# A two-layer attention and mixture-of-experts kernel: routing products of 128 columns, and one token buffer in the first expert stage

## The chip, the cores and the metric

The kernel runs on one core of a Trainium2 chip. The metric is the device time of one execution in microseconds (us). TensorE (PE in the profile) has a clock that is granted to it at one of two levels, 1.2 or 2.4 GHz; the profile prints the granted clock as a share of the full one (0.50 or 1.00). A measurement of this kernel is repeated with the same program, and the three runs before lie within 1.9 us of each other.

## What is computed

The input is `x`, 4 x 512 = 2048 tokens of 512 numbers, and a context of 4 x 512 x 128. Four sublayers are added to the tokens one after the other:

```python
x = x + graph_attention(ctx_512, layernorm(x), ...)
x = x + ffn(layernorm(x), gate, gate_up_proj, down_proj)          # 32 experts, top 4
x = x + attention(q=layernorm(x), k=ctx_512, v=ctx_512)           # 32 heads of 16
x = x + moe(layernorm(x), w_cls, bias, w_gate_up, w_down)         # 32 real + 32 empty experts, top 8, capacity 256
```

In each of the two expert sublayers a token's normalised row is multiplied with a routing matrix (512 x 32 in the first, 512 x 64 in the second), a softmax gives scores, the largest 4 (8) are kept and normalised. Each chosen expert computes `silu(x Wg) * (x Wu)` and a product with its down matrix, and the weighted results are summed into the token.

## The kernel before, in words

The program (`two_layers`) is a chain of stages with a barrier over all engines between them: graph attention (`g_` in tile names), first expert sublayer (`sparse_ffn` with prefix `f`: a stage `route`, tiles `fr_`, and a stage `experts`, tiles `f_`), `attention_prepare` (`p_`), `attention` (`a_`), the second expert sublayer (`sr_` and `s_`), and `copy_out`. Inside a stage each engine has its own instruction list, written out by hand, and waits on semaphores. SP issues plain DMAs, POOL (GpSimd) issues the indirect ones. The running sum of the tokens lives in a DRAM tensor `tokens`.

**`route`** works on 16 tiles of 128 tokens, in 4 groups of 4. DVE computes statistics, ACT and DVE normalise, PE transposes a tile in four pieces (L863, bank `xtb`), ACT copies it to SBUF (L904, `xT`), and PE multiplies the four pieces with the four slices of the routing matrix (L870): the stationary operand is the token tile, the moving one is `gate_sb[:, c, :]` with E = 32 or 64 columns, and the result is the tile's logits in bank `lg`. In the trace such a float32 product of the program shows as two records, a transpose as one. PE's list is: transposes of tile t, then products of tile t-1. After the products of a group DVE takes the maxima (`maxima(g)`, L971), ACT the exponentials, DVE chooses (`choose(g)`) and works out places (`places(g)`). DVE's list in the middle is

```python
maxima(0); maxima(1); choose(0); maxima(2); choose(1); places(0)
maxima(3); choose(2); places(1); choose(3); places(2); weights(); places(3)
```

and then, in the first sublayer, how many tiles of 128 each expert gets (`tiles_of`, at least one), the number of its first tile (`first`), and a table of the expert of each of the 96 tiles, which goes through a PE transpose into row `table`. The last result is `ids`, the token numbers of each tile's 128 places (L1102). Beside that SP stores the normalised rows (`x_rows`), loads the weights of the first four experts and, in the first sublayer only, fills a second DRAM tensor `tokens_odd` with zeros (L816, 4.6 MB).

**`experts`** goes over 96 tiles (first sublayer) or 64 (second, two for each expert: `static`). POOL gathers the rows of a tile by `ids` (L1204), six tiles ahead. PE, ACT and DVE transpose them, do the up product, the activation, the down product; ACT copies the result into one of four buffers `y` (L1311). POOL waits for it (`y_ready`) and for the scatter two tiles back (`added[j % 2]`), and issues an indirect DMA that adds the 128 rows of `y` to DRAM (L1219). Tokens in the tiles of one expert are distinct; those of two experts can be the same, and two such additions must not be under way at once. The first sublayer avoids it with two targets: even tiles are added to `tokens`, odd ones to `tokens_odd`. The second has one target and waits at each even tile (a new expert) for the scatter just before. ACT may write `y` of tile j once the scatter of tile j-4 has landed.

**`attention_prepare`** loads `tokens` and `tokens_odd` in four pairs (L1431, L1432), DVE adds them (L1496), takes statistics (L1499), SP stores the sum back to `tokens` (L1437). After the mean and deviation of all 16 tiles it normalises (L1513), and PE, ACT and DVE transpose each tile and split it into three bf16 parts that SP stores.

Of the kernel before, what the change touches and what calls it, by code (L numbers as in the profile page):

```python
# [11 lines left out]
P = 128  # L12
RING = 2
FP32 = mybir.dt.float32
BF16 = mybir.dt.bfloat16
I32 = mybir.dt.int32
# [601 lines left out]
def sparse_ffn(nc, tokens, tokens_odd, gate, sel_bias, gate_up, down, K, capacity, pre):  # L618
# [5 lines left out]
    RE = 4  # L624
# [4 lines left out]
    with ExitStack() as stack:  # L629
        def sb(name, shape, dt=FP32):  # L630
# [5 lines left out]
            "table": sb("table", [1, 2 * P + NE], I32),  # L636
# [7 lines left out]
        route(nc, tokens, tokens_odd, gate, sel_bias, gate_up, down, x_rows, kept, K, capacity, n_tiles, RE, pre + "r_")  # L644
        experts(nc, tokens, tokens_odd, gate_up, down, x_rows, kept, capacity, n_tiles, RE, pre + "_")


def route(nc, tokens, tokens_odd, gate, sel_bias, gate_up, down, x_rows, kept, K, capacity, n_tiles, RE, pre):
# [17 lines left out]
    XTR = 4  # L666
    ids, table_i, wgu, wd = kept["ids"], kept["table"], kept["wgu"], kept["wd"]
# [3 lines left out]
    with ExitStack() as stack:  # L671
# [25 lines left out]
        gate_sb = sb("gate", [P, DC, E])  # L697
# [30 lines left out]
        passed = sb("passed", [P, ER])  # L728
        expert_of = sb("expert_of", [P, 1])
# [7 lines left out]
        def logits(t):  # L737
            return lg_bank[t // G][:, t % G * E:(t % G + 1) * E]

        def group_logits(g):  # L740
            return lg_bank[g][:, 0:G * E].rearrange("p (t e) -> p t e", t=G)

        def group_pos(g):
            return lg_bank[g][:, 256:256 + G * ER].rearrange("p (t e) -> p t e", t=G)
# [31 lines left out]
        N_CONST = 10  # L776
        with nc.Block() as block:

            @block.gpsimd
            def _(pool):  # L780
# [18 lines left out]
                pool.memset(zeros_e[:, :], 0.0).then_inc(consts, 1)  # L799
                pool.iota(my_slot[:, :], [[P, n_tiles]], base=1, channel_multiplier=1, allow_small_or_imprecise_dtypes=True).then_inc(consts, 1)  # L800

            @block.sync
            def _(sp):
                for g in range(NG):
# [4 lines left out]
                    elif g == 0:  # L809
                        sp.dma_start(gate_sb[:, :, :], gate.rearrange("(c p) e -> p c e", p=P)).then_inc(gate_loaded, 16)  # L810
# [294 lines left out]
def experts(nc, tokens, tokens_odd, gate_up, down, x_rows, kept, capacity, n_tiles, RE, pre):  # L1105
# [17 lines left out]
    with ExitStack() as stack:  # L1123
# [53 lines left out]
        with nc.Block() as block:  # L1177
# [20 lines left out]
            def _(pool):  # L1198
# [9 lines left out]
                for j in range(AHEAD):  # L1208
                    gather(j)
# [761 lines left out]
```

## Time and profile before

| | us |
|---|---|
| median of 3 runs | 2397.76 (2395.94 to 2397.82) |
| the profiled execution, its own time | 2393.21 |
| its span in the trace | 2391.6 |
| PE busy in the span | 1884.6 (79%) |
| DVE busy | 1558.2 (65%) |
| ACT busy | 1113.1 (47%) |
| POOL busy | 575.8 (24%) |
| mean granted clock of TensorE | 0.883 |

A time in the trace counts from the start of the span. A row of the timeline gives start, duration, engine, line, operation, written and read tiles, shape, number of merged instructions, and in brackets how long the engine was idle before and what ended that. A row of a table by stretch gives the stretch, its length, then for each engine the busy time and the number of instructions, then the granted clock, the busy share of the DMA engines and GB/s.

### The profile page before, as it was taken

What the parts mean: (1) busy time and instruction counts of PE and PEld (TensorE: products, weight loads), DVE (VectorE), ACT (ScalarE), POOL (GpSimd) and SP (SyncE); (2) the same over time, 40 slices, a digit from 0 to 9 for tenths busy, and PEclk for the clock granted to TensorE, in tenths of its full rate; (3) what the DMA queues carried; (4) which work ended last, traced back from release to release, by engine and by line L of the source; (5) the groups of instructions that cost most, each with busy time, mean ns of one, the idle gap of its engine ahead of it and who ended that gap; (6) DMA issues with size and microseconds to landing.
All of it is one profiled execution on the core that took longest, in us unless ns stands there. A gap on an engine that the chain in (4) does not pass through costs nothing. (4 is left out here: it accounts for less than half of the span.)

```text
span 2391.6 us, 34851 instructions
## 1 busy us (share of the span) xinstructions
PE 1884.6 (79%) x8270; PEld 919.9 (38%) x8271; DVE 1558.2 (65%) x3296; ACT 1113.1 (47%) x2022; POOL 575.8 (24%) x679
## 2 busy tenths in 40 slices
PE   1898867888567999999982159888889638999994
PEld 0444424444264555555541112222222324454442
DVE  5988969888665555555556257777777394555552
ACT  1988849888432222222222316666666532222221
POOL 3000030001102455454540201111111103444441
PEclk9899877999757999999995569999999768999997
DMA  4101121001364778888558741111111345898984
GB/s 134 39 37 42 35 103 45 36 37 36 107 230 100 172 184 211 210 190 197 106 87 276 130 74 50 53 49 49 49 49 45 128 146 148 229 228 227 232 215 109
DMA packets 207120, 288.47 MB, mean 121 GB/s; under 512 B 83168, under 2 KB 121440, under 8 KB 205920
## 3 DMA queue, kind: packets, MB, share of 16 engines
q1 hardware_dynamic: 168464, 190.16, 26.0%
q0 software_dynamic: 38544, 97.02, 20.3%
q8 instruction: 46, 0.75, 0.1%
q14 instruction: 66, 0.54, 0.1%
HBM read 208.64 MB, written 82.28 MB: 122 GB/s over the span
## 5 line engine op out<-in xcount | busy, mean ns | idle before, releaser
L1829 DVE TENSOR_REDUCE a_negmax<-a_m 128x1 f32<-128x512 f32 x512 | 327.8, 685 | 86.3 <-PE a_m L1694 84.6
L1783 ACT ACTIVATE a_prob<-a_s 128x1024 f32<-128x1024 f32 x256 | 260.2, 1020 | 142.7 <-PE a_s L1705 136.3
L1694 PE MATMUL a_m<-a_kT,a_qT 112*128 (+1 forms) x512 | 198.2, 398 | 115.6 <-DMA a_kT<-k_parts 63.9
L1253 PE MATMUL f_gu_bank<-f_wgu,f_xT 128*128 x768 | 271.2, 496 | 15.7 <-issue 12.1
L354 PE MATMUL g_pt<-g_ident,g_p 128*128 128x128 f32 x1024 | 185.2, 311 | 95.8 <-ACT g_p L460 94.4
L1253 PE MATMUL s_gu_bank<-s_wgu,s_xT 128*128 128x512 f32 x512 | 232.7, 597 | 2.3 <-ACT s_xT L1305 1.6
L354 PEld LDWEIGHTS g_pt<-g_ident,g_p 128*128 128x128 f32 x1024 | 127.2, 155 | 239.2 <-issue 153.5
L460 ACT ACTIVATE g_p<-g_e,g_emin 128x512 f32<-128x512 f32 x256 | 184.2, 719 | 66.0 <-DVE g_emin L554 65.7
L1253 PEld LDWEIGHTS f_gu_bank<-f_wgu,f_xT 128*128 128x128 f32 x768 | 141.5, 191 | 156.3 <-issue 79.7
L544 DVE SCALAR_TENSOR_TENSOR g_l<-g_tb,g_s,g_h 128x512 f32<-128x512 f32 x256 | 189.6, 742 | 16.7 <-ACT g_h L438 16.7
L438 ACT ACTIVATE g_h<-g_tb,g_s 128x512 f32<-128x512 f32 x256 | 182.2, 715 | 3.9 <-DMA g_tb<-neighbours 3.9
L1272 PE MATMUL f_y_bank<-f_wd,f_actT 96*128 x384 | 180.9, 593 | 1.2 <-DVE f_actT L1338 0.9
L554 DVE CUSTOM_DVE_ANT_0 g_e<-g_l,g_mask 128x512 f32<-128x512 f32 x256 | 174.4, 682 | 0.0
L1338 DVE COPY f_actT<-f_at_bank 96x256 f32<-96x256 f32 x96 | 40.4, 421 | 189.6 <-PE f_at_bank L1262 185.2
L1694 PEld LDWEIGHTS a_m<-a_kT,a_qT 112*128 112x128 bf16 x512 | 49.5, 97 | 286.9 <-DVE a_negmax L1829 167.1
L1705 PE MATMUL a_s<-a_qT,a_kT 115*128 115x512 bf16 x512 | 153.3, 382 | 0.4 <-DMA a_qT<-a_mrows 0.2
L1219 POOL DMA_INDIRECT tokens<-s_y,s_ids x64 | 101.5, 1586 | 199.4 <-ACT s_y L1311 195.1
L1253 PEld LDWEIGHTS s_gu_bank<-s_wgu,s_xT 128*128 128x128 f32 x512 | 97.9, 192 | 125.4 <-issue 125.4
L383 PE MATMUL g_o<-g_pT,g_feat 128*64 128x512 f32 x512 | 144.9, 648 | 0.0
L1717 PE MATMUL a_o<-a_prob,a_val 128*32 128x512 f32 x1024 | 136.4, 605 | 0.4 <-ACT a_prob L1783 0.4
L1319 ACT ACTIVATE f_en<-f_gu_bank 128x192 f32<-128x192 f32 x96 | 31.7, 330 | 220.1 <-PE f_gu_bank L1253 220.1
L1351 DVE RECIPROCAL f_den<-f_den 128x192 f32<-128x192 f32 x96 | 129.8, 1353 | 3.3
(290 smaller groups left out, 3005.6 us busy)
## 6 DMA issues: line engine op xcount, KB each, us to landing
s_wgu<-in_L_ffn_w_gate_up SPq DMA_DIRECT2D x32, 1024.0 KB
f_wgu<-in_L_ffn_gate_up_proj SPq DMA_DIRECT2D x32, 768.0 KB
g_tb<-neighbours SPq DMA_DIRECT2D x8, 2048.0 KB
s_wd<-in_L_ffn_w_down SPq DMA_DIRECT2D x32, 512.0 KB
a_qT<-q_parts SPq DMA_DIRECT2D x224, 64.0 KB
f_wd<-in_L_ffn_down_proj SPq DMA_DIRECT2D x32, 384.0 KB
q_parts<-p_part SPq DMA_DIRECT2D x48, 128.0 KB, 2.0
tokens_odd<-fr_zero_row SPq DMA_DIRECT2D x1, 4608.0 KB
```

Source lines behind the costliest of these rows:

```text
L354: last = nc.tensor.transpose(pt_bank[n % BANKS][:, c, :], prob[:, n % LAG, c * P:(c + 1) * P], ident[:, :])
L383: last = nc.tensor.matmul(o_bank[pr % RING][hh * F_OUT:(hh + 1) * F_OUT, :], feat[k % SLOTS][:, c, h * F_OUT:(h + 1) * F_OUT], probT[:, pr ...
L438: nc.scalar.activation(high[:, n % LAG, :], t_all[k % SLOTS][:, h, :], ACT.Relu, scale=-4.0, bias=s_high[k % SLOTS][:, t, h:h + 1]).then_i ...
L460: nc.scalar.activation(prob[:, n % LAG, :], eneg[:, n % LAG, :], ACT.Exp, scale=-1.0, bias=emin[:, n % LAG:n % LAG + 1], accum_out=rsum[:, ...
L544: V.scalar_tensor_tensor(out=lneg[:, n % LAG, :], in0=t_all[k % SLOTS][:, h, :], scalar=s_low[k % SLOTS][:, t, h:h + 1], in1=high[:, n % L ...
L554: V.tensor_tensor_reduce(out=eneg[:, n % LAG, :], in0=lneg[:, n % LAG, :], in1=mask[k % SLOTS][:, local % NT, :], scale=1.0, scalar=3.0e38 ...
L1253: last = nc.tensor.matmul(gu_bank[k % TR][:, 0:F], xT[k % TR][:, c, :], wgu[:, bass.ds(place, 1), c, :].rearrange("p a f -> p (a f)"), sta ...
L1272: last = nc.tensor.matmul(y_bank[k % TR][:, :], actT[k % TR][:, c, :], wd[:, bass.ds(place, 1), c, :].rearrange("p a f -> p (a f)"), start ...
L1694: nc.tensor.matmul(m_bank[n % RING][:, :], qT[k][0:PAIR_ROWS, head, st * P:(st + 1) * P], group_keys(G, PAIR_ROWS, slice(0, N)), start=Tru ...
L1705: last = nc.tensor.matmul(s_bank[n % RING][:, i, :], group_keys(G, ROWS_ALL, slice(tt * P, (tt + 1) * P)), qT[k][0:ROWS_ALL, 2 * pair + i, ...
L1783: nc.scalar.activation(prob[n % QR][:, :, :], s_bank[n % RING][:, :, :], ACT.Exp).then_inc(p_ready, 1)
L1829: V.tensor_reduce(negmax[k % RING][:, st, head:head + 1], m_bank[n % RING][:, :], X_AXIS, ALU.max, negate=True).then_inc(m_read, 1)
```

## The change

It has two parts.

The routing matrix in SBUF (`gate_sb`) becomes 128 columns wide. The columns behind E are set to zero by POOL (one memset more, `N_CONST` 11), and each product at L870 streams all 128, so that a tile's logits and their zeros take 128 columns of the bank, four tiles fill it, and the positions are written over columns 64 to 95 of a tile's part.

`tokens_odd` is gone: the zero fill in `route`, the loads, the 16 additions and the store back in `attention_prepare`. All scatters of the first expert stage go to `tokens`. DVE makes a flag for each tile, 16 if it is the first of an expert and 0 if not (`begins`, `new_here`, one PE transpose more, two more small copies into `table`). POOL reads the flag of tile j into a register before the scatter of j and waits for `added[(j-1) % 2]` to reach that flag plus the count that is long there: for the first tile of an expert the scatter just before must have landed. Tiles 1 and 2 always wait so.

```diff
-        gate_sb = sb("gate", [P, DC, E])
+        gate_sb = sb("gate", [P, DC, P])
...
         def logits(t):
-            return lg_bank[t // G][:, t % G * E:(t % G + 1) * E]
+            return lg_bank[t // G][:, t % G * P:t % G * P + E]
...
+                pool.memset(gate_sb[:, :, E:P], 0.0).then_inc(consts, 1)
...
-                if tokens_odd is not None:
-                    stores += 1
-                    sp.dma_start(tokens_odd.rearrange("(j p) d -> p j d", p=P),
-                                 bass.AP(zero_row, 0, [[D + EXTRA, P], [0, NT + 2], [1, D]])).then_inc(x_stored, 16)
...
-                            last = nc.tensor.matmul(logits(t - 1), xT[:, (t - 1) % XTR, c, :], gate_sb[:, c, :],
+                            last = nc.tensor.matmul(lg_bank[(t - 1) // G][:, (t - 1) % G * P:((t - 1) % G + 1) * P], xT[:, (t - 1) % XTR, c, :], gate_sb[:, c, :],
...
+                    link(V.tensor_scalar(begins[:, :], first[:, :], row_no[:, 0:1], None, ALU.is_equal))
                     V.tensor_reduce(expert_of[:, :], passed[:, 0:ER - 1], X_AXIS, ALU.add).then_inc(expert_ready, 1)
+                    V.tensor_reduce(new_here[:, :], begins[:, :], X_AXIS, ALU.add).then_inc(expert_ready, 1)
...
+                    link(V.tensor_copy(table_i[:, 2 * P + NE:], misc_bank[0:1, P:2 * P]))
+                    link(V.tensor_scalar(table_i[:, 2 * P + NE:], table_i[:, 2 * P + NE:], 4, None, ALU.logical_shift_left))
...
                     pool.wait_ge(y_ready, j + 1)
                     if j >= 2:
-                        pool.wait_ge(added[j % 2], 16 * (j // 2))
+                        pool.wait_ge(added[j % 2], landed(j))
+                    if j in (1, 2) and not static:
+                        pool.wait_ge(added[(j - 1) % 2], landed(j + 1))
+                    if j > 2 and not static:
+
+                        new = pool.value_load(table[0:1, 2 * P + NE + j:2 * P + NE + j + 1])
+                        pool.wait_ge(added[(j - 1) % 2], new + landed(j - 1))
+                        pool.sem_inc(turns_pool, 1)
...
-                    acc = tokens_odd if j % 2 and not static else tokens
...
-                    sp.dma_start(odd[:, g * NT:(g + 1) * NT, :], tokens_odd[g * N:(g + 1) * N, :].rearrange("(t p) d -> p t d", p=P)).then_inc(tok_in[g], 16)
                 sp.dma_start(ctx_sb[:, :, :], ctx_dram.rearrange("b (t p) f -> p (b t) f", p=P)).then_inc(ctx_in, 16)
-                for g in range(B):
-
-                    sp.wait_ge(tok_ready, (g + 1) * NT)
-                    sp.dma_start(tokens[g * N:(g + 1) * N, :].rearrange("(t p) d -> p t d", p=P), tok[:, g * NT:(g + 1) * NT, :]).then_inc(tok_stored, 16)
...
-                    V.tensor_tensor(tok[:, t, :], tok[:, t, :], odd[:, t, :], ALU.add).then_inc(tok_ready, 1)
-                    if t >= 1:
-                        dve.wait_ge(tok_ready, t)
-                        chain.mark(V.bn_stats(stats[:, t - 1, :], tok[:, t - 1, :]))
+                    chain.mark(V.bn_stats(stats[:, t, :], tok[:, t, :]))
```

How it stands in the lists, first PE in `route` of the first sublayer (`fr_xtb` are the transposes, `fr_lg` the logits), before and after:

```order
L863 MATMUL fr_xtb<-f_ident,fr_xn 128x128 x4
L870 MATMUL fr_lg<-fr_gate,fr_xT 128x32 x4
L863 MATMUL fr_xtb<-f_ident,fr_xn 128x128 x4
L870 MATMUL fr_lg<-fr_gate,fr_xT 128x32 x4
L863 MATMUL fr_xtb<-f_ident,fr_xn 128x128 x4
```

```order
L863 MATMUL fr_xtb<-f_ident,fr_xn 128x128 x4
L870 MATMUL fr_lg<-fr_gate,fr_xT 128x128 x4
L863 MATMUL fr_xtb<-f_ident,fr_xn 128x128 x4
L870 MATMUL fr_lg<-fr_gate,fr_xT 128x128 x4
L863 MATMUL fr_xtb<-f_ident,fr_xn 128x128 x4
```

Nothing is moved there; only the moving operand is wider. Then POOL in the first expert stage, from tile 3 on, before and after:

```order
L1219 DMA tokens_odd<-f_y,f_ids 2304x512
L1204 DMA f_row<-f_x_rows,f_ids 128x576
L1219 DMA tokens<-f_y,f_ids 2304x512
L1204 DMA f_row<-f_x_rows,f_ids 128x576
L1219 DMA tokens_odd<-f_y,f_ids 2304x512
```

```order
L1229 TENSOR_LOAD f_table
L1230 REGISTER_ALU
L1234 DMA tokens<-f_y,f_ids 2304x512
L1210 DMA f_row<-f_x_rows,f_ids 128x576
L1229 TENSOR_LOAD f_table
L1230 REGISTER_ALU
L1234 DMA tokens<-f_y,f_ids 2304x512
```

Each scatter has a register load, an addition and one wait more ahead of it, behind the gather of six tiles on. Last SP at the start of `attention_prepare`, before and after:

```order
L1431 DMA p_tok<-tokens 128x4x512
L1432 DMA p_odd<-tokens_odd 128x4x512
L1431 DMA p_tok<-tokens 128x4x512
L1432 DMA p_odd<-tokens_odd 128x4x512
L1431 DMA p_tok<-tokens 128x4x512
L1432 DMA p_odd<-tokens_odd 128x4x512
L1431 DMA p_tok<-tokens 128x4x512
L1432 DMA p_odd<-tokens_odd 128x4x512
L1433 DMA p_ctx<-in_ctx 128x16x128
L1437 DMA tokens<-p_tok 128x4x512 x4
```

```order
L1443 DMA p_tok<-tokens 128x4x512 x4
L1444 DMA p_ctx<-in_ctx 128x16x128
L1451 DMA q_parts<-p_part 128x4x128 x48
```

Four loads and four stores of 1 MB are gone from the queue, and the context's load stands four places earlier.

## Rows read from the trace of the kernel before

**Rows 1.** Busy time by stretch: most of the first routing stage; the first expert stage

```profile
670.00:735.00 65.00, 36.17 (x225) 32.15 (x223) 43.76 (x190) 21.46 (x63) 0.00 (x0) 0.50 0.48 142
735.00:1255.00 520.00, 492.76 (x1728) 271.64 (x1728) 287.88 (x672) 146.33 (x288) 253.90 (x192) 0.99 0.73 166
```

**Rows 2.** Timeline of the first routing stage: TensorE's weight loads (PEld)

```profile
677.55 1.83 PEld L870 LDWEIGHTS fr_lg<-fr_gate,fr_xT 128*128 128x128 f32 x8
...
679.12 0.90 PEld L863 LDWEIGHTS fr_xtb<-f_ident,fr_xn 128*128 128x128 f32 x4
...
680.00 1.83 PEld L870 LDWEIGHTS fr_lg<-fr_gate,fr_xT 128*128 128x128 f32 x8
```

**Rows 3.** Timeline of PE, second routing stage

```profile
1897.38 1.94 PE L870 MATMUL sr_lg<-sr_gate,sr_xT 128*128 128x64 f32 x8
...
1904.87 1.81 PE L870 MATMUL sr_lg<-sr_gate,sr_xT 128*128 128x64 f32 x8
...
1907.31 1.00 PE L870 MATMUL sr_lg<-sr_gate,sr_xT 128*128 128x64 f32 x8
...
1908.60 1.00 PE L870 MATMUL sr_lg<-sr_gate,sr_xT 128*128 128x64 f32 x8
```

**Rows 4.** Short stretches: second routing stage, then first expert stage (clock third from the end)

```profile
1907.00:1908.00 1.00, 1.00 (x10) 1.00 (x9) 0.21 (x1) 0.49 (x1) 0.00 (x0) 0.85 0.75 277
...
746.00:747.00 1.00, 1.00 (x3) 0.53 (x2) 0.00 (x0) 0.00 (x0) 0.00 (x0) 0.62 0.78 253
```

**Rows 5.** Timeline of PE at the start of the first expert stage: 384-column products

```profile
742.02 5.17 PE L1253 MATMUL f_gu_bank<-f_wgu,f_xT 128*128 x8 [1.20 <-ACT f_xT L1305]
```

**Rows 6.** Timeline of DVE, first routing stage

```profile
686.99 0.29 DVE L971 TENSOR_REDUCE fr_negmax<-fr_lg 128x4 f32<-128x128 f32 x1 [6.64 <-PE fr_lg L870]
...
692.29 2.49 DVE L1018 TENSOR_TENSOR fr_low_hot<-fr_count_h,fr_low 128x512 f16<-128x512 f16 x4
696.22 0.29 DVE L971 TENSOR_REDUCE fr_negmax<-fr_lg 128x4 f32<-128x128 f32 x1 [1.44 <-PE fr_lg L870]
```

**Rows 7.** Timeline of DVE in the second routing stage, the third maxima

```profile
1918.70 0.42 DVE L971 TENSOR_REDUCE sr_negmax<-sr_lg 128x4 f32<-128x256 f32 x1 [1.14 <-PE sr_lg L870]
```

**Rows 8.** Timeline, first loads and statistics: first routing stage, then prepare

```profile
642.91 0.39 SPq L805 DMA_DIRECT2D fr_tok<-tokens  x1
...
648.86 2.47 DVE L953 BATCH_NORM_STATS2 fr_stats<-fr_tok 128x6 f32<-128x512 f32 x4 [5.71 <-DMA fr_tok<-tokens]
...
1265.23 0.39 SPq L1431 DMA_DIRECT2D p_tok<-tokens  x1
...
1273.68 1.29 DVE L1496 TENSOR_TENSOR p_tok<-p_tok,p_odd 128x512 f32<-128x512 f32 x2 [27.40 <-DMA p_odd<-tokens_odd]
...
1289.95 0.69 DVE L1496 TENSOR_TENSOR p_tok<-p_tok,p_odd 128x512 f32<-128x512 f32 x1 [0.58 <-DMA p_odd<-tokens_odd]
...
1295.45 1.17 DVE L1504 BATCH_NORM_AGGREGATE p_mv<-p_stats 128x2 f32<-128x6 f32 x16
...
1297.39 1.46 DVE L1513 TENSOR_SCALAR p_xn<-p_tok,p_mv,p_rstd 128x512 f32<-128x512 f32 x3
```

**Rows 9.** Timeline of POOL: first expert stage, its last scatter, and second expert stage

```profile
759.56 1.64 POOL L1219 DMA_INDIRECT tokens<-f_y,f_ids  x1 [14.53 <-ACT f_y L1311]
761.51 1.08 POOL L1204 DMA_INDIRECT f_row<-f_x_rows,f_ids  x1 [0.31 <-issue]
764.52 1.59 POOL L1219 DMA_INDIRECT tokens_odd<-f_y,f_ids  x1 [1.93 <-ACT f_y L1311]
...
1251.82 1.55 POOL L1219 DMA_INDIRECT tokens_odd<-f_y,f_ids  x1 [0.72 <-ACT f_y L1311]
...
2051.43 1.59 POOL L1219 DMA_INDIRECT tokens<-s_y,s_ids  x1 [4.02 <-DMA tokens<-s_y,s_ids]
```

**Rows 10.** Register loads from the table by PE's queue: count, min/median/max ns

```profile
L1235 PEldq TENSOR_LOAD <-f_table x192: 294/307/1000, 740.3 to 1247.8; - x192
```

**Rows 11.** A short stretch at the end of the first expert stage

```profile
1256.00:1257.00 1.00, 0.00 (x0) 0.00 (x0) 0.00 (x0) 0.00 (x0) 0.00 (x0) 0.50 0.00 0
```

More of the change, by code:

```diff
@@ L615, with sparse_ffn @@
 PAD = 4
-def sparse_ffn(nc, tokens, tokens_odd, gate, sel_bias, gate_up, down, K, capacity, pre):
+def sparse_ffn(nc, tokens, gate, sel_bias, gate_up, down, K, capacity, pre):
     T, D = 2048, 512
@@ L635, in sparse_ffn @@
             "ids": sb("ids", [P, n_tiles], U32),
-            "table": sb("table", [1, 2 * P + NE], I32),
+            "table": sb("table", [1, 3 * P + NE], I32),
             "wgu": sb("wgu", [P, RE, D // P, F]),
@@ L643, in sparse_ffn, with route @@
         }
-        route(nc, tokens, tokens_odd, gate, sel_bias, gate_up, down, x_rows, kept, K, capacity, n_tiles, RE, pre + "r_")
-        experts(nc, tokens, tokens_odd, gate_up, down, x_rows, kept, capacity, n_tiles, RE, pre + "_")
-def route(nc, tokens, tokens_odd, gate, sel_bias, gate_up, down, x_rows, kept, K, capacity, n_tiles, RE, pre):
+        route(nc, tokens, gate, sel_bias, gate_up, down, x_rows, kept, K, capacity, n_tiles, RE, pre + "r_")
+        experts(nc, tokens, gate_up, down, x_rows, kept, capacity, n_tiles, RE, pre + "_")
+def route(nc, tokens, gate, sel_bias, gate_up, down, x_rows, kept, K, capacity, n_tiles, RE, pre):
     T, D = 2048, 512
@@ L842, in positions @@
                         pe.wait_ge(mask_ready, t + 1)
-                        out = lg_bank[g][:, 256 + t % G * ER:256 + (t % G + 1) * ER]
+                        out = lg_bank[g][:, t % G * P + 2 * ER:t % G * P + 3 * ER]
                         nc.tensor.matmul(out, before[:, :], mask[:, t, :], start=True, stop=False)
@@ L884, in _ @@
                     nc.tensor.matmul(misc_bank[:, 0:ER], ones[:, :], mask_sum[:, NT, :], start=True, stop=True).then_inc(count_ps, 1)
-                    pe.wait_ge(expert_ready, 1)
+                    pe.wait_ge(expert_ready, 2)
+                    nc.tensor.transpose(misc_bank[0:1, 128:128 + P], new_here[:, :], ident[:, :])
                     nc.tensor.transpose(misc_bank[0:1, 256:256 + P], expert_of[:, :], ident[:, :]).then_inc(expert_ps, 1)
@@ L914, in _ @@
                     act.wait_ge(gate_ps, 1)
-                    nc.scalar.activation(gate_sb[:, :, :].rearrange("p c e -> p (c e)"), misc_bank[:, 0:DC * E], ACT.Copy).then_inc(gate_ready, 1)
+                    nc.scalar.activation(gate_sb[:, :, 0:E], misc_bank[:, 0:DC * E].rearrange("p (c e) -> p c e", c=DC), ACT.Copy).then_inc(gate_ready, 1)
                 for t in range(NT + 2):
@@ L1102, in _, with experts @@
                 link(V.scalar_tensor_tensor(out=ids[:, :], in0=tab_bank[:, 0:n_tiles], scalar=-1.0, in1=blank[:, :], op0=ALU.add, op1=ALU.add))
-def experts(nc, tokens, tokens_odd, gate_up, down, x_rows, kept, capacity, n_tiles, RE, pre):
+def experts(nc, tokens, gate_up, down, x_rows, kept, capacity, n_tiles, RE, pre):
     NE, D, F = gate_up.shape
@@ L1209, in _, with landed @@
                     gather(j)
+                def landed(j):
+                    return 16 * (j // 2)
                 for j in range(n_tiles):
@@ L1374, with attention_prepare @@
 ROWS_ALL = PAIR_ROWS + PARTS
-def attention_prepare(nc, tokens, tokens_odd, ctx_dram, q_parts, k_parts):
+def attention_prepare(nc, tokens, ctx_dram, q_parts, k_parts):
     B, N, CF = ctx_dram.shape
@@ L1942, in two_layers @@
     graph_attention(nc, x, ctx_512, W0, a_self0, a_neigh0, b0, W1, a_self1, a_neigh1, b1, neighbours, tokens)
-    sparse_ffn(nc, tokens, tokens_odd, gate, None, gate_up_proj, down_proj, 4, None, "f")
-    attention_prepare(nc, tokens, tokens_odd, ctx_512, q_parts, k_parts)
+    sparse_ffn(nc, tokens, gate, None, gate_up_proj, down_proj, 4, None, "f")
+    attention_prepare(nc, tokens, ctx_512, q_parts, k_parts)
     attention(nc, tokens, ctx_512, q_parts, k_parts)
-    sparse_ffn(nc, tokens, None, w_cls, bias, w_gate_up, w_down, 8, 256, "s")
+    sparse_ffn(nc, tokens, w_cls, bias, w_gate_up, w_down, 8, 256, "s")
     copy_out(nc, tokens, out)
```

29 lines of the change are left out of this document (13 added, 16 removed).

## The prediction

> **What bounds the kernel now.** I read the busy table by stretches first, since each stage ends in a barrier and a saving in one goes straight into the end, unless the stage has another chain. In the first expert stage TensorE is busy 492.8 of 520 us at a clock of 0.99 [rows 1]: there nothing that POOL does counts while TensorE is fed. In the first routing stage TensorE has the clock 0.50 throughout [rows 1], and its queue is one row of weight loads: the eight for a tile's products begin at 677.55, the four for the next transposes at 679.12, the next products' at 680.00 [rows 2]. So a tile takes 2.45 us and a load 0.204 us. DVE waits for those products: 6.64 us before the second-to-last but one group's maxima and 1.44 us before the last's, at 696.22 [rows 6]. From there DVE's list runs on to the end of the stage. The second routing stage has the same list with 64 columns. There the products begin at 1897.38 and a tile takes 2.44 us too (1904.87 to 1907.31) until the clock rises: 0.85 in the microsecond from 1907 [rows 4], the upper level from about 1907.3; then a tile takes 1.29 us [rows 3]. In `attention_prepare` DVE waits until 1273.68 for the first pair of loads and works through 16 additions and statistics until 1295.45 [rows 8]. The chain of waits is of less use here, as it names the second expert stage only.
>
> **Wider products, first routing stage.** What does a product of 128 columns cost? The eight records with 384 columns take 5.17 us at half clock [rows 5], 0.646 us each, so 0.215 us for 128 columns. A weight load has 0.204 us anyway [rows 2]. The padding thus costs 8 x 0.011 = 0.1 us a tile at the low clock, 1.4 us over 16, and about nothing at the upper one, where both halve. I book it at nothing because of what follows; the cover is the weight load, and without it the price would be 0.16 us a record (rivals).
>
> What it may bring is the clock. With 32 columns it never rose in 40 us of gapless weight loads; with 64 it rose 9.9 us after the first products; with 384 columns the products began at 742.02 [rows 5] and the clock rose within the microsecond from 746 (0.62, so at about 746.8) [rows 4], 4.7 us after. 128 columns keep the array streaming almost as long as the loads take (0.215 of 0.215), which is nearest to the third case. I take 4.7 us after the first products of this stage, which begin two tiles and a little before the third tile's: the third tile's products would begin at 662.8, with the clock up. In the second routing stage the eight tiles after the rise, up to the third maxima at 1918.70 [rows 7], took 11.4 us, ACT's work and table load in them. Here ten tiles are left to that point: 11.4 + 2 x 1.29 = 14.0, so the third maxima come at 676.8, not 686.99. From there DVE is the bound: from the third maxima to the end of the first `places` it takes 686.99 to 692.29 + 2.49 = 694.78, 7.8 us [rows 6], so the fourth maxima are at 684.6 in place of 696.22, and wait no longer for PE. After that DVE's list is as before. **-11.6 us.** Bounds: clock up one tile earlier, -12.9; as late as in the second routing stage (9.9 us), fourth maxima at 687.0, -9.2.
>
> Added on DVE are two small operations of 32 columns before the flags' transpose, each less than the 0.29 us of the 128-column maxima [rows 6]; two table copies fall into a wait for PE at the stage's end. Together +0.4 us. One memset on POOL ends long before PE starts: nothing. The zero fill of 4.6 MB leaves SP's queue; the loads behind it are not what DVE waits for: nothing.
>
> **Second routing stage.** If the clock rises 4.7 us after 1897.38, at 1902.1, tiles 3 and 4 take 1.29 instead of 2.44: **-2.2 us** (0 to -3.5). The third maxima wait for PE there (1.14 us [rows 7]), and all that DVE does behind them moves along.
>
> **Prepare.** In the first routing stage four loads of 1 MB are issued in the same way: 642.91 to the first statistics at 648.86 is 5.95 us [rows 8]. So here statistics start at 1265.23 + 5.95 = 1271.2. Pairs of loads followed one another every (1289.95 - 1273.68) / 3 = 5.4 us, so a load every 2.7 us: the last group is in at 1279.3, and four statistics (2.47 [rows 8]) end at 1281.7. From the end of the statistics to the first normalisation it is 1297.39 - 1295.45 = 1.94 us: 1283.7 against 1297.39, **-13.7 us** (-12.4 if the first group saves only half a pair's pitch, -14.5 if DVE alone sets it). 16 tiles' normalisation and splitting go on as before, 13.7 us earlier; the store back of `tokens` hid beside them and is just gone.
>
> **First expert stage.** POOL's own work for a tile is 1.59 + 0.3 + 1.06 + 0.3 = 3.3 us against a shortest interval of 4.96 (759.56 to 764.52) [rows 9]: 1.7 us are free. A register load by PE's queue takes 0.307 us [rows 10]; POOL's is not in the trace, and I take the same: 3.6 us. The Trainium skill puts the floor of a tensor load at about 600 ns (DMA: Bandwidth & Descriptors, Latency and other measured facts). By that POOL would need 3.9 us, still under 4.96, and the last scatter of the stage would be 0.3 us later still.
>
> New waits: 31 tiles begin an expert. A scatter alone lands within 4.2 us of its start by my reading of the stage's end (it starts at 1251.82 [rows 9], and the DMA engines are quiet from 1256 on [rows 11]); between weight loads one held POOL until 2051.43, 4.02 us of waiting [rows 9], some 7 us. So a boundary may hold a scatter back by up to 2 us, and behind it a gather that is six tiles early; ACT needs the buffer of four tiles before, 20 us old. POOL catches up 1.4 us in each tile after it. Queue and buffers hide it: nothing for the waits, **+0.3 us** for the load ahead of the last scatter. Bounds: 0 and +5.
>
> **Sum.** -11.6 + 0.4 - 2.2 - 13.7 + 0.3 = -26.8 us. On the profiled execution's 2393.2 it gives 2366.4. That execution was 4.6 us under the median, 2397.8, from which I count: **2371.0 us**.
>
> **Rivals.**
> - *The clock stays down.* 128 columns do to the grant what 32 did. For it: in the middle of the first routing stage the queue is just as gapless and the clock still 0.50 [rows 1, 2]. Against it: 64 columns were enough in the end. Then -13.7 + 0.4 + 0.3 + 1.4 = -11.6: 2386.2. This is also the case in which the padding doesn't do its work. Chance 0.12.
> - *A product costs its columns on top of its load.* Then a record of 128 columns costs 0.16 us more than one of 32 at the low clock: 128 x 0.16 = 20 us in the first routing stage, 7 us in the second, against the clock's gain. It speaks against it that 32 and 64 columns have one pace, 2.45 and 2.44 us a tile [rows 2, 3]. Total about -13.7 - 13.8 + 27 = 0: 2397. Chance 0.02. By the Trainium skill (TensorE: Matmul & The Clock Gate, Wait — 56ns, not 53.3ns?) matmuls follow each other in exactly N / 1.2 GHz while cold, which makes 107 ns of 27; the trace's tiles of equal pace do not agree for these float32 products.
> - *POOL becomes the bound (slower).* If a scatter takes L us to land, 31 tiles cost L + 0.6 and 65 cost 3.6 on POOL. They pass TensorE's 5.2 us a tile once L is over 8; at L = 10 it is +60 us in the expert stage, in sum +33: 2431. For it: all scatters now go to one tensor, and one wait of 4.02 us shows that landing can be late [rows 9]. Against it: in the second expert stage every second scatter waits in this way at more DMA load, and only this one wait was for a DMA. Chance 0.04.
> - *Late landings reach TensorE now and then*, a few boundaries in a row with weights loading: +5 to +10, 2378. Chance 0.10.
>
> **How the numbers follow.** My case has 0.72: 2371.0, with its own range of 2366 to 2377 from the bounds. The clock case at 2386 and the late landings at 2378 make up most of the rest. For 8 in 10 I take 2364 to 2384, which leaves out the clock case's middle, POOL as the bound and the equal case. This kernel's measurement can tell 0.2%, 4.8 us. Faster by more: 0.94; within it: 0.02; slower: 0.04.
>
> **What would show it.** Stretches of the first routing stage with a clock of 1.00 from about 663 to 682, products eight in 1.0 us, and the fourth maxima near 685 without a wait; the second routing stage's clock up at about 1902 in the old count, its end 2 us shorter; 12 us from the first statistics to the normalisation in prepare; in the first expert stage 520 us as before, with waits for DMA on POOL under 2 us at some 31 scatters. The forecast is wrong in its main step if the granted clock in the first routing stage is still 0.50 at its last products, and wrong in the other if ACT's copies of `y` wait for a scatter.

## The result and the profile after the change

The changed kernel takes 2356.88 us (median of 4 runs, 2356.2 to 2363.82); the kernel before takes 2396.99 us in the same comparison (2395.94 to 2397.82). The ratio is 0.9839, 95% interval 0.982 to 0.9858: 40.1 us faster where 26.8 were forecast, and under the range's low end of 2364. The profiled execution took 2357.2 us, its span 2355.6 us (2391.6 before, so 36.0 less; the profiled execution of before lay 3.8 us under its median). Lengths of stages here and below are of one profiled execution for each kernel; where a change left a stage alone, they differ by 1 to 4 us from trace to trace.

Each stage begins with a marked event (its first load, its first gather, its first normalisation), and the difference of two of them gives its length in either trace:

| stretch | before | after | difference | forecast |
|---|---|---|---|---|
| graph attention, to 642.91 / 645.31 | 642.9 | 645.3 | +2.4 | 0 |
| first routing, to the first gather | 93.1 | 81.6 | -11.4 | -11.2 |
| first experts, to the first load of prepare | 529.3 | 519.3 | **-9.9** | **+0.3** |
| prepare, to the first normalisation | 32.2 | 18.9 | -13.3 | -13.7 |
| rest of prepare, and attention | 582.1 | 582.8 | +0.7 | 0 |
| second routing | 99.6 | 95.7 | -3.9 | -2.2 |
| second experts and the end | 412.5 | 411.9 | -0.6 | 0 |

The terms of the first routing stage and of prepare came as forecast, that of the second routing stage in kind. One stage that was to stay as it was lost 9.9 us.

Stretches of the changed kernel (columns as in [rows 1]); they answer to [rows 1] and [rows 4]:

```profile
660.00:727.00 67.00, 33.57 (x286) 28.74 (x284) 53.01 (x223) 27.45 (x73) 0.07 (x1) 0.68 0.49 143
726.93:1246.26 519.33, 490.54 (x1728) 274.74 (x1728) 289.55 (x672) 146.31 (x288) 254.12 (x192) 0.97 0.74 167
663.00:664.00 1.00, 1.00 (x7) 1.00 (x6) 1.00 (x2) 0.60 (x1) 0.00 (x0) 0.61 0.09 27
...
1868.00:1869.00 1.00, 1.00 (x8) 1.00 (x7) 1.00 (x3) 0.07 (x1) 0.00 (x0) 0.66 0.02 8
```

The clock (third from the end) comes up at about 663.8 in the first routing stage, 3.4 us after the first products at 660.40, and at about 1868.7 in the second, 4.1 us after 1864.54. The products themselves (timeline of PE, against [rows 2, 3]):

```profile
660.40 2.08 PE L870 MATMUL fr_lg<-fr_gate,fr_xT 128*128 128x128 f32 x8
662.27 1.06 PE L863 MATMUL fr_xtb<-f_ident,fr_xn 128*128 128x128 f32 x4
663.13 1.38 PE L870 MATMUL fr_lg<-fr_gate,fr_xT 128*128 128x128 f32 x8
...
664.78 1.06 PE L870 MATMUL fr_lg<-fr_gate,fr_xT 128*128 128x128 f32 x8
665.67 0.60 PE L863 MATMUL fr_xtb<-f_ident,fr_xn 128*128 128x128 f32 x4
666.11 1.06 PE L870 MATMUL fr_lg<-fr_gate,fr_xT 128*128 128x128 f32 x8
```

At the upper level a tile takes 1.33 us (664.78 to 666.11); the one whole tile at the lower level takes 2.73 (660.40 to 663.13). The third and the fourth maxima (timeline of DVE, against [rows 6]):

```profile
679.09 0.29 DVE L972 TENSOR_REDUCE fr_negmax<-fr_lg 128x4 f32<-128x128 f32 x1 [2.14 <-PE fr_lg L870]
...
684.38 2.50 DVE L1019 TENSOR_TENSOR fr_low_hot<-fr_count_h,fr_low 128x512 f16<-128x512 f16 x4
686.80 0.29 DVE L972 TENSOR_REDUCE fr_negmax<-fr_lg 128x4 f32<-128x128 f32 x1
```

The third come 18.7 us after the first products (18.8 forecast), the fourth 7.7 later (7.8 forecast) and no longer wait for PE. Prepare (timelines of SP's queue and of DVE, against [rows 8]):

```profile
1246.26 2.97 SPq L1443 DMA_DIRECT2D p_tok<-tokens  x4
...
1252.06 2.47 DVE L1502 BATCH_NORM_STATS2 p_stats<-p_tok 128x6 f32<-128x512 f32 x4 [26.77 <-DMA p_tok<-tokens]
...
1260.71 2.47 DVE L1502 BATCH_NORM_STATS2 p_stats<-p_tok 128x6 f32<-128x512 f32 x4 [0.31 <-DMA p_tok<-tokens]
...
1265.17 1.46 DVE L1514 TENSOR_SCALAR p_xn<-p_tok,p_mv,p_rstd 128x512 f32<-128x512 f32 x3
```

The statistics begin 5.8 us after the first load (5.95 forecast), their four groups take 11.1 us (10.5 forecast), and 2.0 us lie behind them (1.9).

**Where the 9.9 us are.** The new waits are there, and some are larger than forecast. The waits of POOL in the first expert stage (us in total, times, longest):

```profile
POOL tokens L1234 <- DMA tokens<-f_y,f_ids: 163.5, 65, 5.9
```

That row must be read with care. It gives the whole idle time of POOL ahead of a scatter and names the semaphore that moved last. In the kernel before, the same view puts 18 scatters down to a landing in the other tensor, for which none of them waits. The real waits can be found otherwise: 32 scatters of the changed kernel start 0.82 to 0.85 us behind the landing of the one before. The forecast had 31.

What the edit did to nearly every scatter is something else. A tile of the kernel before, ACT's copy of `y` and the scatter that takes it (timelines of ACT and of POOL):

```profile
815.65 0.60 ACT L1311 ACTIVATE f_y<-f_y_bank 128x512 f32<-128x512 f32 x1 [1.12 <-PE f_y_bank L1272]
816.53 1.58 POOL L1219 DMA_INDIRECT tokens_odd<-f_y,f_ids  x1 [2.00 <-DMA tokens<-f_y,f_ids]
```

A tile of the changed kernel; the scatter ahead of it lands at about 817.2, so this one did not wait for that landing:

```profile
815.27 0.60 ACT L1326 ACTIVATE f_y<-f_y_bank 128x512 f32<-128x512 f32 x1 [1.12 <-PE f_y_bank L1287]
817.12 1.58 POOL L1234 DMA_INDIRECT tokens<-f_y,f_ids  x1 [2.00 <-DMA tokens<-f_y,f_ids]
```

The scatter starts 0.28 us behind the end of the copy before, and 1.25 us behind it after; between the two lies the load of the flag, begun at 815.9:

```profile
L1229 POOLq TENSOR_LOAD <-f_table x1: 287/287/287, 815.9 to 815.9; - x1
```

In the kernel before all 96 scatters start within 0.5 us of the end of their copy; in the changed kernel 95 of 96 start over 0.9 us behind it, and the latest of them, held by landings, up to 6.0 us.

The waits of ACT in the same stretch; six copies of `y` did wait for a scatter:

```profile
ACT f_y L1326 <- DMA tokens<-f_y,f_ids: 7.5, 6, 1.5
```

TensorE nevertheless runs closer. The waits of PE in that stage, kernel before:

```profile
PE f_gu_bank L1253 <- issue: 12.1, 30, 1.1
```

The same line of the changed kernel:

```profile
PE f_gu_bank L1268 <- issue: 3.6, 5, 1.1
```

"issue" ahead of the up product is time in which the array had nothing because its queue had not got so far. In this stage the queue reads two registers from `f_table` ahead of each up and each down product. All loads of line 1234, kernel before (count, min/median/max ns; those of line 1235 are [rows 10]):

```profile
L1234 PEldq TENSOR_LOAD <-f_table x192: 296/310/1087, 739.7 to 1246.9; - x192
```

The same of the changed kernel, with the flags' loads on POOL's queue:

```profile
L1249 PEldq TENSOR_LOAD <-f_table x192: 296/303/1052, 730.6 to 1226.0; - x192
L1250 PEldq TENSOR_LOAD <-f_table x192: 294/304/1006, 731.2 to 1226.4; - x192
L1229 POOLq TENSOR_LOAD <-f_table x93: 283/290/992, 765.8 to 1231.9; - x93
```

The median before is 0.31 us, the largest 1.09. I listed all 384 loads of PE with their starts: 101 took over 0.5 us before, 18 after. A piece of the kernel before shows one of the 101 (the loads in a short window):

```profile
L1234 PEldq TENSOR_LOAD <-f_table x1: 877/877/877, 813.7 to 813.7; - x1
```

POOL's timeline around it:

```profile
811.57 1.58 POOL L1219 DMA_INDIRECT tokens<-f_y,f_ids  x1 [2.49 <-ACT f_y L1311]
813.46 1.06 POOL L1204 DMA_INDIRECT f_row<-f_x_rows,f_ids  x1 [0.31 <-issue]
```

And PE's:

```profile
810.50 2.75 PE L1253 MATMUL f_gu_bank<-f_wgu,f_xT 128*128 x8
813.08 0.38 PE L1262 MATMUL f_at_bank<-f_ident,f_act 128*96 128x128 f32 x2
813.30 0.60 PE L1243 MATMUL f_xt_bank<-f_ident,f_row 128*128 128x128 f32 x4
813.73 1.88 PE L1272 MATMUL f_y_bank<-f_wd,f_actT 96*128 x4
815.81 2.84 PE L1253 MATMUL f_gu_bank<-f_wgu,f_xT 128*128 x8 [0.19 <-issue]
```

The load for the next up product begins at 813.7, 2.1 us behind the scatter's start and 0.2 us behind the gather's, and ends with that gather; the up product comes 5.31 us after the last one. The 95 intervals from one up product to the next say it for the whole stage: before, 2 of them are 4.97 us or less; after, 42 are. From the first to the last up product it is 497.0 us before and 485.2 after. So almost every tile of the kernel before was later than it could have been, 48 of them by about 0.1 us, in which no idle time shows. But those make little of the sum: counted from 4.96 us up, 9.7 of the 11.8 us lie in the intervals over 5.1 us, of which there are 45 before and 25 after.

### The profile page after: what moved, and what is told of

It reads as the page before. It is cut to its first block and busy times, and to the rows that moved or that the text cites. A ratio compares the mean times of both kernels' runs of the same rounds, so it can differ in the third digit from the quotient of the medians.

```text
span 2355.6 us, 35114 instructions
## 1 busy us (share of the span) xinstructions
PE 1865.1 (79%) x8271; PEld 905.3 (38%) x8272; DVE 1551.9 (66%) x3284; ACT 1112.6 (47%) x2022; POOL 576.9 (24%) x681
## 5 line engine op out<-in xcount | busy, mean ns | idle before, releaser
L1830 DVE TENSOR_REDUCE a_negmax<-a_m 128x1 f32<-128x512 f32 x512 | 328.1, 686 | 86.3 <-PE a_m L1695 84.7
L1234 POOL DMA_INDIRECT tokens<-f_y,f_ids x96 | 152.1, 1584 | 224.5 <-DMA tokens<-f_y,f_ids 163.5
L285 POOL DMA_DIRECT2D tokens<-g_xo x16 | 12.1, 756 | 496.7 <-DVE g_xo L591 492.7
```

The lines of the kernel that those rows point to most:

```text
L1234: pool.indirect_dma_start(out=tokens, out_offset=bass.IndirectOffsetOnAxis(ap=ids[:, j:j + 1], axis=0), in_=y[j % YR][:, :], in_offset=Non ...
L1830: V.tensor_reduce(negmax[k % RING][:, st, head:head + 1], m_bank[n % RING][:, :], X_AXIS, ALU.max, negate=True).then_inc(m_read, 1)
```

## The experiments

My first theory was: **POOL's issue of a gather slows PE's register loads; the new waits moved the gathers.** The rivals: the padding brought it; one target of the scatters is quicker; slow loads are a symptom. All runs are compared with the kernel before on the same chip; stage lengths are of the profiled executions, counted as above.

**e1, e2: the two halves of the change.** e1 is the change without its edits to tokens, flags and waits, e2 without its padding:

```
-    gate_sb = sb("gate", [P, DC, E])
+    gate_sb = sb("gate", [P, DC, P])            (e1; e2 the reverse)
...
-    matmul(logits(t - 1), xT..., gate_sb[:, c, :])
+    matmul(lg_bank[..][:, (t-1)%G*P:((t-1)%G+1)*P], xT..., gate_sb[:, c, :])
```

> The kernel before with the wider routing products alone (two token buffers and no flags kept). Theory (the gap of 9.9 us in the first expert stage comes from the waits on POOL, which moved its gathers off PE's register loads): first routing stage -11.5 us, second -4, first expert stage unchanged at about 529 us with some 100 of PE's register loads over 0.5 us, prepare unchanged at 32 us; in sum -15, so about 2382. Rival (the routing stage's end, or the clock, sets how the expert stage starts, and the padding brought the 9.9 us too): expert stage 519, sum -25, about 2372.

> The change without the wider products: one token buffer, flags and waits kept, routing products as before. Theory: first routing stage about 93 us as before, first expert stage about 519 us with fewer than 30 slow register loads, prepare 19 us, second routing stage 99.6; sum -9.9 -13.3 = -23, so about 2374. Rival (the padding brought the 9.9 us): expert stage 529, sum -13, about 2384.

e1: 2382.84 us, ratio 0.9942 (0.9929 to 0.9955); first routing 81.5, first experts 531.5, prepare 32.2, second routing 97.3. e2: 2369.25 us, 0.9894 (0.9878 to 0.9911); 93.6, 517.5, 18.2, 97.1. The halves add up (0.9942 x 0.9894 = 0.9837), and the padding has no part in the expert stage. Second routing stages without padding took 96.0 to 100.2 us in the profiles of this study, with it 94.8 to 97.3: the change gives some 2.5 us there, as forecast, and part of the 3.9 is scatter.

**e3, e4: the waits alone, and the gather's place alone.** e3 has flags and waits but both buffers; e4 is the kernel before with one step moved:

```
     for j in range(n_tiles):
-        if j + AHEAD < n_tiles:
-            gather(j + AHEAD)
         pool.wait_ge(y_ready, j + 1)
+        if j + AHEAD < n_tiles:                 (first expert stage only)
+            gather(j + AHEAD)
```

> The kernel before with the flags and the waits on POOL alone; both token buffers are kept, the scatters go to two tensors in turn, and prepare adds them up. Theory (timing of POOL): the gathers move off PE's register loads all the same, the first expert stage takes about 519 us with fewer than 30 loads over 0.5 us; sum -9.5, so about 2387.5. Rival (scatters to one tensor are what is quicker): expert stage stays at 529 us, 2397.5 with the flags' work. Second rival (the waits cost, and the one buffer paid for it): over 530 us, over 2398.

> The kernel before with one thing moved in the first expert stage: POOL issues the gather for six tiles on after it has waited for y and ahead of the scatter, not behind the scatter. No wait is added. Theory (a gather's issue on POOL slows PE's register loads beside it, and only those ahead of the next up product reach the end): the gather now falls where the loads behind a running up product lie, so loads over 0.5 us may stay many, but PE's idle time before the up products falls from 12.1 us to under 4, the stage takes 518 to 520 us, and the kernel about 2387.5. Rival (slow loads are a symptom, or the waits or the single buffer brought the time): 529 us, no difference, 2397.

e3: 2384.34 us, 0.9953 (0.9939 to 0.9968), stage 516.0 us. The flags and waits bring the time with two targets too, so the single buffer is not what does it. Here 94 of 96 scatters start over 0.9 us behind their copy. e4: 2375.41 us, 0.9913 (0.9899 to 0.9926), stage **509.2 us**: one moved line gives 20 us in this stage, twice what I expected. It has neither flag nor landing wait, but the gather now stands between the copy and the scatter, and 90 of 96 scatters start over 1.3 us behind their copy. It also spoke against my theory. 174 of PE's loads began beside a gather in e4, and none was slow. Sorted by the time since the last *scatter's* start, the loads of all traces fall in place (table below): of those that begin 1.9 to 3.0 us behind it most are slow, of the others hardly any. In the kernel before a gather follows 1.9 us behind each scatter but the last ones, so the two could not be told apart. New theory: **the scatter slows the loads some time behind its start; the gather is innocent.** By it the order, the flag and the waits work in one way: they put the scatter a microsecond or more later, and PE's loads, which keep their place, then begin too soon behind it to be slowed. Loads that begin in those 1.9 to 3.0 us are 139 before, 36 in the changed kernel, 5 in e4.

**f6 and its control f0: the gather moved away, the scatter left.** f6 is the kernel before, with a wait of POOL for ACT's copy of the next x ahead of the gather. From here on the kernels carry bounds on the register loads that feed waits, which put two more short instructions behind one of PE's two loads for each product; f0 is the kernel before with these alone.

```
+    pool.wait_ge(xt_ready, min(j + 4, n_tiles))   (f6)
     if j + AHEAD < n_tiles: gather(j + AHEAD)
...
-    e = pe.value_load(table[0:1, bass.ds(j, 1)])
+    e = pe.value_load(table[0:1, bass.ds(j, 1)], min_val=0, max_val=NE - 1)   (f0, f6)
```

> The kernel before; in the first expert stage POOL issues its gather behind the scatter as before, but first waits for ACT's copy of the next x (xT), about 2 us later, so that the gather's issue falls behind PE's register loads, while the scatter stays where it was (bounds on the register loads as in the run beside it). Theory A (the scatter itself slows the register loads that begin 1.9 to 3.0 us behind its start; the gather is innocent): still about 100 loads over 0.5 us, now without a gather beside them, stage about 529 us, kernel about 2397. Theory B (the gather's issue slows them): slow loads gone, stage 509 to 512, kernel about 2378. Theory C (only a gather right behind a scatter): as B.

> The kernel before with bounds on PE's and SP's register loads in the expert stage: two short instructions more behind the first of PE's two loads for a product, about 0.3 us of queue time by the gap between the loads in f5 (0.6 us in place of 0.3 to 0.5). Control for f6. Theory (PE's queue between a down product and the next up product is on the path whenever a load there is slow): the stage grows from 529 us by 96 x 0.3 = up to 29 us at most, about 545 to 556; f6 (554.8) then differs little from it, so that the gather's place is worth nothing by itself. Rival (queue time is hidden, and f6's 26 us are the late gather's own cost): 529 to 532.

f6: 2420.84 us, 1.0107 (1.0091 to 1.0123), stage 554.8; f0: 2422.98 us, 1.0109 (1.0093 to 1.0124), 555.3. The forecast of f6's time left the bounds out; against its control the gather's place is worth nothing, and its slow loads are as many (81 and 79). One of them in f6 (the loads in a short window):

```profile
L1236 PEldq TENSOR_LOAD <-f_table x1: 971/971/971, 807.8 to 807.8; - x1
```

By POOL's timeline of f6 it begins 2.35 us behind the scatter and is over before the gather begins:

```profile
805.45 1.58 POOL L1221 DMA_INDIRECT tokens<-f_y,f_ids  x1 [0.75 <-ACT f_y L1313]
809.21 1.06 POOL L1204 DMA_INDIRECT f_row<-f_x_rows,f_ids  x1 [2.17 <-ACT f_xT L1307]
```

And f0 shows the second half of the mechanism: the gap between the two loads of a product grows from 0.16 to 0.45 us, and the stage by 26 us of 529, so PE's queue is on the path.

The slow loads also share an end. In f0, f6 and the kernel before, those that begin 2.2 to 2.5 us behind the scatter take 0.92 or 0.93 us in the median and those that begin 2.5 to 2.8 us behind it 0.68 to 0.70, so that both kinds end about 3.3 us behind the scatter's start. It looks as if they were held until then; what holds them no run shows.

**f7: what of the scatter?** As f0, with the scatters of this stage writing without adding; the sum over a token's four experts is left out.

```
-    compute_op=ALU.add
+    compute_op=ALU.add if static else ALU.bypass
```

> f0_before_bounded (the kernel before with bounds on its register loads, 2423 us, stage 555.3), and the scatters of the first expert stage write their rows without adding to what is there (the sum over a token's four experts is left out). Theory A1 (the adding in the scatter's transfer slows the loads): of some 89 loads that begin 1.9 to 3.0 us behind a scatter's start hardly one is slow (84 in f0), stage 530 us or less. Theory A2 (a scatter's transfer or its descriptors as such): 80 or more slow, stage about 555.

2398.77 us, 1.001 (1.0001 to 1.0019), by the ratios 24 us less than f0; stage 533.2, 3 over what I gave it, and 11 slow loads in place of 79. It is scatters that add which slow the loads. Their issue is also 0.56 us shorter without the adding (1.02 us against 1.58), so the harmful time could merely have moved forward by as much; but of the 74 loads that begin 1.34 to 2.44 us behind a scatter here only 11 are slow. Whether it is the adding in the transfer or something in its issue stays open.

| kernel | loads 1.9 to 3.0 us behind a scatter's start: slow of all | all others: slow of all | up products 4.97 us or less apart | stage, us |
|---|---|---|---|---|
| before | 96 of 139 | 5 of 245 | 2 | 529.3 |
| changed | 18 of 36 | 0 of 348 | 42 | 519.3 |
| e3 | 13 of 25 | 4 of 359 | 45 | 516.0 |
| e4 | 3 of 5 | 0 of 379 | 60 | 509.2 |
| f0 | 78 of 89 | 1 of 295 | 1 | 555.3 |
| f6 | 81 of 91 | 0 of 293 | 1 | 554.8 |
| f7 | 8 of 105 | 3 of 279 | 6 | 533.2 |

(slow: over 0.5 us; counted from a listing of every load and every scatter of the trace, loads to 0.1 us; with exact starts the counts of all loads in the window are somewhat lower, 127 before, 32 changed, 18 in e3, those over 0.5 us change by one at most)

**f5 and its control f8, f9 to f11: a faster kernel.** f8 is the changed kernel with bounds, f5 the same with the gather first. f9 is f5 with one load in place of two, f10 keeps the number for the down product, f11 is f10 with the gather behind the scatter again:

```
     e = pe.value_load(...)
-    place = pe.value_load(table[0:1, bass.ds(j + P, 1)])
-    return e, place
+    return e, e % RE                              (f9)
...
+    if again and k in kept_e:                     (f10: down product)
+        return kept_e[k], kept_e[k] % RE
```

> The changed kernel, and in its first expert stage POOL issues the gather ahead of the waits for landings and of the scatter (the register loads also get bounds, two short instructions each on the queue of their engine). Theory (only register loads of PE that begin about 2 to 3 us behind a scatter's start are slow, and the order moves both pairs of loads out of it): the first expert stage falls from 519.3 to 509 to 511 us, no more than 5 loads over 0.5 us, the kernel to about 2347. Rival (the waits have already taken what there was): 519, 2357. Second rival (the gather ahead makes the scatter 1.4 us later, and with the waits for landings ACT's copies of y now wait for a free buffer): 520 to 530 us, 2357 to 2368.

> The changed kernel with the same bounds (on POOL's load too). Control for f5. Theory: the first expert stage grows from 519 to 535 to 548 us, and f5 (540.0) is not slower than this. Rival (f5's 540 us are the gather-first order's own cost on the changed kernel, because scatters come later): 519 to 525.

> As f5_change_gather_first, and PE loads one register in place of two ahead of each product (the place in the ring is worked out from the expert's number). One load of 0.3 us goes where the bounds put 0.3 us, so the queue is as long as in the changed kernel itself. Theory (queue time ahead of the up product is what f5 lost): the stage falls from 540 to 509 to 514 us, kernel 2347 to 2352, faster than the changed kernel. Rival (order gather-first is itself bad beside the flag waits): it stays over 530.

> As f9_one_load, and the down product two tiles on uses the expert's number that the up product loaded, but for two tiles in eight: 96 + 26 loads of PE instead of 192. Theory: TensorE's array bounds the stage at 4.95 us a tile, 508 to 511 us; where slow loads still reach the end in f9 they go here: up to 4 us less than f9, kernel about 2346. Rival (reading a register late costs as much): as f9.

> f10_kept_register with the gather behind the scatter again, as in the changed kernel. Theory 1 (with one load and no more ahead of an up product there is slack for a slow one): about 504 to 507 us in the stage, kernel as f10, 2342. Theory 2 (the gather's place is needed, since slow loads of up to 1.1 us still reach the up product): 510 to 519, kernel 2348 to 2356.

f8: 2385.08 us, 0.9955 (0.994 to 0.9971), stage 544.1; f5: 2380.31 us, 0.9933 (0.9921 to 0.9945), stage 540.0. My forecast for f5 failed, since it had the bounds at nothing, and it has 23 slow loads where I gave it no more than 5; against f8, which has 33, the order is worth 4 us in the stage. f9: 2346.33 us, 0.9794 (0.978 to 0.9809), stage 508.7, 89 intervals at 4.97 or less. f10: **2341.89 us, 0.9775 (0.976 to 0.979)**, stage 503.7, 4 under the low end of what I gave it; f11: 2344.51 us, 0.9795 (0.9781 to 0.9808), 504.5. f10 and f11 differ by less than their spread: with 118 loads in place of 384 it doesn't matter where the gather stands, though 12 of f10's loads are still slow. f9 to f11 also carry the changed kernel's edits. So one load fewer for each product is worth 31 us of the stage with bounds (f5 to f9), and f10 beats both kernels, the changed one by some 15 us (by the ratios; they were timed in different sessions). Its first expert stage (busy time by stretch):

```profile
725.90:1229.59 503.69, 479.33 (x1728) 276.57 (x1728) 287.88 (x672) 146.31 (x288) 254.17 (x192) 0.98 0.76 172
```

**f12: the lag of the clock.** f10 with 64 columns in the first routing stage:

```
-    gate_sb = sb("gate", [P, DC, P])
+    gate_sb = sb("gate", [P, DC, P if zero_experts else 64])
```

> f10_kept_register with routing products of 64 columns in place of 128 in the first routing stage (128 stay in the second). Theory (the lag between first products and the upper clock goes with the columns, 9.9 us with 64 in the second routing stage before): clock up at about 670 to 671 in place of 663 to 664, first routing stage 83.8 us (81.4 in f10), kernel 2 to 3 us over f10. Rival (the lag is set by when the stage begins, not by its columns): 81.4, no difference. Second rival (at the low clock 64 columns hide under the weight load and 128 do not, 2.45 against 2.73 us a tile): 81.0.

2341.83 us, 0.9775 (0.9762 to 0.9788). In its profiled execution the clock is still 0.50 in the microsecond from 676 and up in the next, 17.2 us after the first products at 659.79, and the stage takes 86.3 us:

```profile
676.00:677.00 1.00, 1.00 (x7) 1.00 (x7) 0.00 (x0) 0.48 (x1) 0.00 (x0) 0.50 0.00 0
677.00:678.00 1.00, 1.00 (x11) 1.00 (x10) 0.00 (x0) 0.72 (x3) 0.00 (x0) 0.99 0.59 227
```

That is neither the 9.9 us expected nor no difference. This execution, 2347.78 us, was the slowest of its five, and the others (2341.5 to 2343.3) are as fast as f10's. The second routing stages of the other traces show that with 64 columns the lag varies from run to run. From the first products to the upper clock it is 5.1 us (f7), 7.4, 7.6, 7.6, 9.9 (before), 12.6 and 15.1 us (e4). With 128 columns it is 1.1 to 4.4 us in all fifteen routing stages that have them, and with 32 the clock did not come up in any of the seven. The lag shows in the time: the stage takes 96.0 us in f7 and 100.2 in e4.

## Why the prediction was right and wrong, by its steps

- **First routing stage, -11.6 + 0.4.** Measured -11.4. The clock rose 3.4 us after the first products (4.7 taken from [rows 5]), and a tile at the low clock takes 2.73 us rather than 2.54 (2.45 + 0.09); with so few such tiles both are small, and DVE's list then bounds as forecast. In the seven traces with padding the lag was 3.0 to 3.7 us in this stage, so that the term came out near was not the luck of one run.
- **Second routing stage, -2.2.** Measured -3.9, some 2.5 by the mean of the profiles: right in kind and size. The 9.9 us of [rows 4] that I counted from is one draw of a lag between 5.1 and 15.1 us, so that it came near owes something to luck.
- **Prepare, -13.7.** Measured -13.3, each of its three steps within 0.7 us.
- **First expert stage, +0.3: the step that failed**, at "TensorE is busy 492.8 of 520 us ...: there nothing that POOL does counts while TensorE is fed". I costed what POOL's waits would hold up through semaphores and buffers, and found it hidden. That held in the main: the scatters held by a landing were 32 against 31, but with POOL's catching up behind them some came up to 6.0 us after their copy, not under 2, and ACT did wait 6 times, for 7.5 us in all, which I had named as a sign of being wrong. What I left out is that POOL's scatters reach PE in another way, through the duration of its register loads, and that 492.8 us of busy time contain a queue that comes late at nearly every tile. The flag's load and the waits put the scatters 0.9 us or more later, and fewer loads fell where they are slowed (36 in place of 139): -9.9 in place of +0.3. How much of it the load of the flag brings and how much the waits, no run separates. The row was in my hands: [rows 10] ends in a largest load of 1000 ns beside a median of 307, and I read the median alone. My own working had an interval of 4.96 us and a mean of 5.2 us a tile side by side, and I did not ask what lay between. (The 4.96 us were not the shortest interval of the scatters either; one of 4.66 stands in the trace.)
- **The +0.3 us for POOL's register load.** I took PE's 0.307 us; the load itself took about that, but with the addition and the wait behind it the scatter starts 0.9 to 1.0 us later, at the last tile too (1.20 us behind its copy). The term was a third of what it should have been. The floor of about 600 ns that the Trainium skill states (DMA: Bandwidth & Descriptors, Latency and other measured facts) does not agree with this trace, where the load took 0.290 us.
- **The landing of a scatter.** I read 4.2 us at the stage's end. In the changed kernel it took 4.5 us at least, 5.0 in the median and 8.2 at most (from issue to landing, first expert stage), and the scatter that waited started 0.8 us behind that (timeline of POOL, changed kernel):

```profile
751.08 1.64 POOL L1234 DMA_INDIRECT tokens<-f_y,f_ids  x1 [15.08 <-ACT f_y L1326]
753.02 1.08 POOL L1210 DMA_INDIRECT f_row<-f_x_rows,f_ids  x1 [0.31 <-issue]
756.77 1.59 POOL L1234 DMA_INDIRECT tokens<-f_y,f_ids  x1 [2.67 <-DMA tokens<-f_y,f_ids]
```

So the usual landing is well under the 8 us of the rival in which POOL becomes the bound; single ones reach it, and the rival did not come.
- **The rivals.** The clock did rise; products of 128 columns cost 0.28 us a tile more at the low clock (2.73 against 2.45), not the 1.3 (8 x 0.16) of the rival. No rival had the expert stage faster, so the range, built from the bounds 0 and +5 of this term, ended too high. A bound below nothing was missing: I excluded a gain without giving a reason.

## What to carry to other kernels

Where an engine's queue reads registers from memory for each tile, look at the largest of these loads and at the interval between tiles, not at busy time and median; an interval above its own shortest value is money, with or without visible idle time. Read one number and work the others out in registers, or keep it until its second use: here 15 us beyond the change, for a few lines. And when a wait seems to speed a kernel up, ask what it moved: twice the gain in this stage was had by moving one line, without any wait. Last, count a wait only where the code has it: the profile names what moved last, not what was waited for.

## What the runs showed of the hardware

- A register load of PE takes 0.30 us, but many that begin 1.9 to 3.0 us behind the start of an indirect scatter that adds to DRAM take 0.5 to 1.15 us (96 of 139 in the kernel before, 81 of 91 in f6), and end about 3.3 us behind that start. Loads beside a gather's issue alone are not slowed (174 of 174 in e4). Some of POOL's loads are long too (10 of 93 over 0.5 us, largest 992 ns, changed kernel).
- Such a scatter lands 4.5 to 8.2 us behind its start, 5.0 in the median (96 in the changed kernel).
- A register load on POOL with an addition and a wait against its result puts the scatter behind it 0.97 us later (1.25 us behind the copy in place of 0.28), though the load itself takes 0.29.
- Without the adding a scatter of the same rows is issued in 1.02 us and not 1.58, and 11 of 384 loads are slow (f7).
- Bounds on a loaded register (two short instructions, 0.29 us more between two loads) cost 26 us over 192 loads here, since they stand on a queue that is on the path (f0).
- The clock rose 1.1 to 4.4 us after the first routing products with 128 columns (15 stages), 5.1 to 17.2 us after them with 64 (8 stages), and not at all in the stage with 32 (7 stages).
